# Attention block: first weighted sum in one piece, maxima split by ScalarE and Pool, turn moved from step three to step five

## The reference, cut to what matters

```python
x = x + 0.5 * ffn(layernorm(x), ...)
x = x + attn(layernorm(x), Wq, bq, Wk, bk, Wv, bv, Wo, bo)
x = x + 0.5 * ffn(layernorm(x), ...)
# attn: 32 query heads, 8 key/value heads (4 query heads share one), head size 16
Q, K = rope(Q, K)
scores = einsum('bhqd,bhkd->bhqk', Q, K) / sqrt(16)
w = softmax(scores, axis=-1)
out = einsum('bhqk,bhkd->bhqd', w, V) @ Wo.T + bo
```

## Time and profile before

| | before |
|---|---|
| median of 3 runs | 3099.67 us (3096.92 to 3100.73) |
| the profiled execution | 3102.39 us, of which 3100.6 us is the span |
| mean granted TensorE clock | 0.982 |
| TensorE busy | 2960.6 us, 95% |
| VectorE busy | 1890.7 us, 61% |
| ScalarE busy | 1731.7 us, 56% |
| Pool busy | 749.6 us, 24% |
| attention, first reduction to last output copy | 1005.0 to 2262.3 us |

### The profile page before, as it was taken

One profiled execution on the slowest core, in us unless ns is written; L12 is line 12 of the kernel. 1 busy time (PEld: TensorE's weight loads), 2 busy tenths in 40 slices (PEclk: granted clock), 3 DMA queues, 4 the chain that ended last, 5 costly groups with the idle time before them and its releaser, 6 DMA issues. The chain is left out here.

```text
span 3100.6 us, 61131 instructions
## 1 busy us (share of the span) xinstructions
PE 2960.6 (95%) x20310; PEld 1213.7 (39%) x20310; DVE 1890.7 (61%) x2349; ACT 1731.7 (56%) x3156; POOL 749.6 (24%) x644
## 2 busy tenths in 40 slices
PE   7889999999998999999999999999997999999999
PEld 4444444444564122222222222222233444444444
DVE  7853222221676999999999999999723222222221
ACT  5733333333111599999999999999910333333332
POOL 0154444444443000000000000000022444444444
PEclk9999999999999799999999999999998999999999
DMA  4311110011333011111111111111256011111100
GB/s 132 116 43 41 41 41 14 26 41 42 92 106 102 11 34 31 30 30 30 31 31 30 30 30 30 30 31 31 95 181 227 5 42 41 41 41 41 41 14 28
DMA packets 163902, 160.56 MB, mean 52 GB/s; under 512 B 62552, under 2 KB 100824, under 8 KB 163808
## 3 DMA queue, kind: packets, MB, share of 16 engines
q1 hardware_dynamic: 163808, 159.30, 17.4%
HBM read 111.48 MB, written 47.19 MB: 51 GB/s over the span
## 5 line engine op out<-in xcount | busy, mean ns | idle before, releaser
L1756 DVE TENSOR_REDUCE at_neg_max<-at_max_ps 128x1 f32<-128x1024 f32 x1024 | 1172.6, 1206 | 19.8 <-PE at_max_ps L1634 19.0
L1742 ACT ACTIVATE at_probs<-at_score_ps 128x512 f32<-128x512 f32 x2048 | 1112.9, 597 | 81.9 <-PE at_score_ps L1654 37.8
L1663 PE MATMUL at_out_ps<-at_probs,at_v 128*32 128x256 f32 x8192 | 655.0, 391 | 24.4 <-ACT at_out L1728 24.0
L1634 PE MATMUL at_max_ps<-at_km,at_q 48*128 48x512 f16 x2048 | 633.0, 390 | 13.9 <-PEq L1227 8.2
L1654 PE MATMUL at_score_ps<-at_q,at_ks 50*128 50x512 f16 x2048 | 622.0, 382 | 15.0 <-DMA at_q<-at_max_parts 9.3
L983 DVE SCALAR_TENSOR_TENSOR f_h<-f_up_ps,hr_factor,f_gate 128x512 f32<-128x512 f32 x128 | 96.1, 751 | 478.1 <-ACT f_gate L1057 475.9
L1945 POOL TENSOR_TENSOR rows<-rows,bias 128x512 f32<-128x512 f32 x32 | 39.5, 1265 | 1353.2 <-ACTq L1880 1272.8
L1654 PEld LDWEIGHTS at_score_ps<-at_q,at_ks 50*128 50x128 f16 x2048 | 164.4, 93 | 434.8 <-ACT at_probs L1742 394.7
L413 DVE SCALAR_TENSOR_TENSOR f_h<-f_up_ps,hr_factor,f_gate 128x512 f32<-128x512 f32 x112 | 83.9, 749 | 393.9 <-PE f_up_ps L752 240.8
L1663 PEld LDWEIGHTS at_out_ps<-at_probs,at_v 128*32 128x32 f32 x8192 | 161.6, 108 | 402.1 <-issue 219.7
L1057 ACT ACTIVATE f_gate<-f_gate_ps 128x512 f32<-128x512 f32 x128 | 76.4, 597 | 354.3 <-PE f_up_ps L1130 354.3
(11 more groups left out here) (148 smaller groups left out, 3722.5 us busy)
## 6 DMA issues: line engine op xcount, KB each, us to landing
rows<-x SPq DMA_DIRECT2D x40, 1024.0 KB, 5.6
x<-rows SPq DMA_DIRECT2D x16, 1024.0 KB, 4.6
f_raw<-units SPq DMA_DIRECT2D x48, 256.0 KB, 2.6
at_q<-qk_parts SPq DMA_DIRECT2D x384, 32.0 KB, 1.7
rows<-x SPq DMA_DIRECT2D x32, 256.0 KB, 2.8
at_q<-at_max_parts SPq DMA_DIRECT2D x512, 1.0 KB
att<-at_out SPq DMA_DIRECT2D x256, 32.0 KB
out<-rows SPq DMA_DIRECT2D x8, 1024.0 KB, 4.2
```

The lines of the kernel that those rows point to most:

```text
L1634: done = nc.tensor.matmul(max_ps[u % 2][:, half * QB:(half + 1) * QB], q[k][rows, j // SLOTS, h * QB + c * P:h * QB + (c + 1) * P], km[k][ ...
L1663: last = nc.tensor.matmul(out_ps[2 * HD * j:2 * HD * (j + 1), cols], v[k][:, kc, :], probs[:, kc % PBUF, j, cols], start=(kc == 0 and part ...
L1742: nc.scalar.activation(probs[:, kc % PBUF, j, :], score_ps[pos % RING][:], ACT.Exp, scale=HD ** -0.5).then_inc(exps, 1)
L1756: nc.vector.tensor_reduce(neg_max[:, h, column:column + 1], max_ps[u % 2][:], AX.X, ALU.max, negate=True).then_inc(maxed, 1)
```

## The change

Four edits.

1. The first step's sum of a block is issued in one piece behind the fourth unit of step kc = 1 (before: one part behind its second, one behind its fourth unit). Its wait for `out_copied` moves with it.
2. ScalarE's copy of the previous block's output stands before unit 5 (before: unit 4).
3. The split leaves VectorE. ScalarE copies the turned maxima, scaled, from the bank into a new SBUF tile `max_rows` (16 x 2 x 128, f32) and increments `m_copied`; Pool, which did nothing in the attention, makes the high part and then the low part from it. TensorE's reuse of the bank waits for ScalarE's copy alone; SP's `store_max` waits for Pool.
4. The turn stands before unit 16 (before: unit 8).

ScalarE's last group is written out behind its loop, since it has one turn less.

```diff
-TURN_AT = 2
+TURN_AT = 4
@@ scores
-                    pe.wait_ge(m_split, n + 2)
+                    pe.wait_ge(m_copied, n + 2)
@@ run of TensorE
-                            elif kc >= 1:
-                                if kc == 1 and i == 1:
-                                    pe.wait_ge(out_copied, n + 1)
+                            elif kc == 1 and i == 3:
+                                pe.wait_ge(out_copied, n + 1)
+                                weigh(n, k, 0, 0)
+                                weigh(n, k, 0, 1)
+                            elif kc >= 2:
                                 weigh(n, k, kc - 1, i // 2)
@@ Pool, new
+            for m in range(NG * NB):
+                h = m % NB
+                pool.wait_ge(m_copied, m + 1)
+                nc.gpsimd.tensor_copy(max_parts[:, h, 0, :], max_rows[:, h, :]).then_inc(m_high, 1)
+                pool.wait_ge(m_high, m + 1)
+                nc.gpsimd.tensor_tensor(max_parts[:, h, 1, :], max_rows[:, h, :], max_parts[:, h, 0, :],
+                                        ALU.subtract).then_inc(m_split, 1)
@@ ScalarE
+            def copy_maxima(m, h, ps):
+                act.wait_ge(m_turned, m + 1)
+                if not (isinstance(m, int) and m < NB):
+                    act.wait_ge(m_split, m - 1)
+                nc.scalar.activation(max_rows[:, h, :], ps[0:MU, 0:P], ACT.Copy, scale=1.0 / ANCHOR).then_inc(m_copied, 1)
+
+            copy_maxima(0, 0, score_ps[0])
@@ run of ScalarE
-                            if unit == GH and not (isinstance(n, int) and n == 0):
+                            if unit == GH + 1 and not (isinstance(n, int) and n == 0):
                                 copy_output(n - 1, 1 - h, (G if h else G - 1) * (GH * 32) + 1)
                             act.wait_ge(s_done, n * SU + (unit + 1))
                             nc.scalar.activation(probs[:, kc % PBUF, j, :], score_ps[pos % RING][:], ACT.Exp,
                                                  scale=HD ** -0.5).then_inc(exps, 1)
+                            if unit == TURN_POS and (h == 0 or follow >= 1):
+                                copy_maxima(n + 1, 1 - h, score_ps[TURN_POS % RING])
@@ VectorE
-            def split_maxima(m, h, ps):
-                dve.wait_ge(m_turned, m + 1)
-                nc.vector.tensor_scalar(max_parts[:, h, 0, :], ps[0:MU, 0:P], 1.0 / ANCHOR, None,
-                                        ALU.mult).then_inc(m_high, 1)
-                dve.wait_ge(m_high, m + 1)
-                nc.vector.scalar_tensor_tensor(out=max_parts[:, h, 1, :], in0=ps[0:MU, 0:P], scalar=1.0 / ANCHOR,
-                                               in1=max_parts[:, h, 0, :], op0=ALU.mult,
-                                               op1=ALU.subtract).then_inc(m_split, 1)
```

More of the change, by code:

```diff
@@ L1537, in attention @@
         out = sb("out", [P, NB, QB], F32)
+        max_rows = sb("max_rows", [MU, NB, P], F32)
         anchor = sb("anchor", [2, T], F16)
@@ L1548, in attention @@
         m_turned = sem("m_turned")
+        m_copied = sem("m_copied")
         m_high = sem("m_high")
@@ L1714, in _ @@
                 weigh(NG * NB - 1, 1, KC - 1, part)
+        @block.gpsimd
+        def _(pool):
+            for m in range(NG * NB):
[5 more added lines that the diff above has]
+                                        ALU.subtract).then_inc(m_split, 1)
         @block.scalar
         def _(act):
+            def copy_maxima(m, h, ps):
[4 more added lines that the diff above has]
+            copy_maxima(0, 0, score_ps[0])
             for semaphore, count in before:
@@ L1743, in run @@
                                                  scale=HD ** -0.5).then_inc(exps, 1)
+                            if unit == TURN_POS and (h == 0 or follow >= 1):
+                                copy_maxima(n + 1, 1 - h, score_ps[TURN_POS % RING])
             run(0, 0, 0, 2)
-            with loop(nc, act, 1, NG) as G:
+            with loop(nc, act, 1, NG - 1) as G:
                 run(G, 0, 0, 2)
+            run(NG - 1, 0, 0, 0)
             copy_output(NG * NB - 1, 1, (NG - 1) * (GH * 32) + 1)
@@ L1772, in _ @@
                 for u in range(MU):
-                    if m == 1 and u == 2:
-                        split_maxima(0, 0, score_ps[0])
                     maxima(m, m, u)
@@ L1780, in run @@
                     for u in range(MU):
-                        if u == TURN_AT * MSTEP and (h == 0 or follow >= 1):
-                            split_maxima(n + 1, 1 - h, score_ps[TURN_POS % RING])
                         if follow >= 1:
```

## The result

| | before | after |
|---|---|---|
| median (12 runs each) | 3100.89 us | 3106.38 us |
| lowest to highest | 3096.74 to 3104.39 | 3099.18 to 3111.75 |
| the profiled execution | 3102.39 us, span 3100.6 | 3107.25 us, span 3105.4 |

The ratio is 1.0016, with a 95% interval of 1.0009 to 1.0024: the change makes the kernel some 5.5 us slower. I had forecast 3092.8 us in a range from 3083 to 3105; the median lies 1.4 us above that range.

A forecast was written before the change was run, and what follows sets the result against it. Even blocks were held bound by SP's issues, so only shorter odd blocks help in groups 2 to 29. Terms 5.6 + 0.7 + 0.1 + 0.5 = 6.9 us gave 3095.5, against the median 3092.8; range 3083 to 3105.

The forecast's parts named there:

- no gain or loss by itself: Odd block, turn moved before unit 16: the same matmul, still 0.21 us, so nothing gained or lost.
- Pool's path through SP: Odd block: Pool's pair, SP's 8 issues (4.94 us) and landing end at 17.7 of 18.70 us, hidden with 0.97 spare.
- The sum of the loop: Odd blocks 0.20 us shorter, 18.90 to 18.70, even blocks unchanged; 28 odd blocks give 5.6 us.
- Merged sum: Odd block, units 4 to 8: sum in one piece with the later output copy gains 0.07 us.
- The stall at the sum: TensorE's 0.40 us wait for ScalarE's output copy stays, moved to behind unit 7.
- The rival that it goes: TensorE's stall at the first sum vanishes: up to 0.40 us more in 34 blocks, 3079 us; chance 0.12, shared with shorter even blocks.
- Copy of the maxima: Odd block: ScalarE's copy takes 0.233 us and holds unit 18 to 1.19 behind unit 16, a loss of 0.05.
- the rival of a long copy: ScalarE's copy of the maxima takes up to 0.59 us, holding unit 18 longer: about 3104.5 us; chance 0.14.
- The 0.08 us in units 10 to 16: Odd block, units 10 to 16: excess, put at 0.06 us in the forecast, goes with the split off VectorE.
- The pace of 1.13: Odd block's last six pairs run at VectorE's 1.13 us; split off VectorE makes them 1.11, gaining 0.12.
- a slow Pool: Odd block: Pool's pair takes over 1.7 us, delaying SP's maxima DMAs; at 2.3 about 3111 us; chance 0.10.
- Pool holding up VectorE: Reductions stand still while Pool works, 0.7 us a block; time about 3105 us; chance 0.04.

The follow-up runs named there:

- a_loop: The changed kernel with ScalarE's last group back in its loop and one unread turn more in the last block; 3096.52 us, 0.9986 of before.
- b_peel: The kernel before with only ScalarE's last group written out behind its loop; 3102.53 us, 1.0007 of before.
- a_turn2: The changed kernel with the turn back before unit 8; 3102.70 us, 1.0009 of the kernel before.
- b_turn4: The kernel before with only the turn moved to before unit 16; 3101.80 us, 1.0006 of before.
- b_sum: The kernel before with only the first sum in one piece and ScalarE's output copy before unit 5; 3091.66 us, 0.9973 of before.
- b_split: The kernel before with the split moved to ScalarE and Pool, plus one unread turn in the last block; 3097.89 us, 0.9992 of before.
- b_km_late: The kernel before with SP's key loads for the maxima issued behind the odd block's maxima DMAs; 3083.66 us, 0.9942 of before.
- a_loop_early: The changed kernel, ScalarE's last group in its loop and its copy of the maxima ahead of unit 16's exponential; 3090.19 us, 0.9967 of before.

## Why the prediction was wrong, and where it was right

**The step that failed first: ScalarE's last group, costed at nothing.** The description of the change names it in one sentence ("written out behind its loop"), and my part by part does not have it at all: the sum puts blocks 62 and 63 at 0.1 us gained. It cost 9.9 us (a_loop against the changed kernel, block 63 at 20.56 against 30.46). Of these some 5.4 us are TensorE's wait and the rest the half clock behind it. That writing the group out brings the pause is shown both ways, by a_loop and b_peel. That it is a transfer of code rests on the q14 transfer in each of the three pauses, in b_peel with no other traffic beside it. The pause lasts 5.80 us here against 3.59 and 2.75 because the transfer begins late: 4.0 us into the pause, against 2.1 and 1.2, while from its start to ScalarE's next instruction it is 1.5 to 1.8 us in all three. Why it begins so late is open. SP's loads for the next stage kept the DMA engines about half busy until 2255.2, just when it begins, and b_peel's and a_turn2's pauses did not meet them; no run tests that. Block 62, written out too, has no pause; the pause's place in the code says where it falls, and no run says why there.

**The second: the turn with "no gain or loss by itself", and Pool's path through SP "hidden", with 4.94 us for SP's issues everywhere.** Both held in the loop (b_turn4), where SP had a microsecond to spare as forecast. (The terms shown give 18.70 - 17.68 = 1.02 us to spare, not 0.97.) In block 1 the same 8 issues take 7.5 us, a row of the trace of before that I had not read, since I took block 19 for all. Block 1 takes 1.9 us more for it (1.1 the turn, 0.8 ScalarE and Pool) and block 2, with the clock, 0.7: 2.6 of the 3.7 us of blocks 0 to 3. Of the other 1.1 us, block 0 has 1.3 more, with its full clock 2.1 us later, and block 3 gives 0.2 back. Why SP issues more slowly there no run shows. My sum had neither block 0 nor the clock in it.

**The sum of the loop was right, its terms less so.** Odd blocks gained 0.24 us (forecast 0.20), even ones became 0.05 longer (forecast 0), blocks 4 to 59 gained 5.5 us (forecast 5.6). The two belong together: SP's chain starts at an odd block's last scores, and from there to the next odd block it is 20.24 us before and 20.23 after. Only the stretch from an odd block's first to its last scores counts, and that fell by 0.19 us (17.88 to 17.69); I had counted TensorE's last pair in full.
- Merged sum: from unit 4 to 8 took 2.55 us without the turn, forecast 2.62: the gain is 0.14, not 0.07. The sum follows the copy after 0.05 us and not 0.13. But its true worth is what it does behind unit 8, and alone it is 0.37 (b_sum): I had followed the stall on TensorE and not asked who starves during it.
- The stall at the sum stayed, as I claimed: TensorE's weight loads wait for the output copy 63 times, 0.4 us each. The rival that it goes falls.
- Copy of the maxima: 0.25 us, forecast 0.233, so the rival of a long copy falls; unit 18 comes 1.22 behind unit 16, forecast 1.19. The next pair is late too, 1.18, which I did not have.
- The 0.08 us in units 10 to 16 are not a gain of the split's move: they stay in b_split, which has no split on VectorE. They go where the turn goes (b_turn4: 3.32 there without the turn, and 1.18 in units 18 to 20 in its place). The pace of 1.13 went as forecast, but b_sum shows that it needed no move of the split.
- Pool: 0.28 + 0.42 = 0.70 us, forecast 0.72; SP's issues 11.56 us into block 19, forecast 11.6. The rivals of a slow Pool and of Pool holding up VectorE fall: the three reductions beside Pool's pair in block 19 last 1.22 us each, which is also their mean over the kernel. The Trainium skill's factor of two against VectorE (GPSIMD Engine Reference, Engine selection) is for operations with two inputs, and my estimate of 1.1 us took it for both. It is not reached at this size: the one with two inputs takes 0.42 against VectorE's 0.28, a factor of 1.5, the other 0.28 against 0.27. VectorE read PSUM there and Pool SBUF.
- The even block is bound by SP: b_km_late shows it by 17 us.

**The small stages.** The stretch to block 0 gained 0.4 us (forecast 0.5), block 3 and blocks 60 to 62 together 0.4 (forecast 0.7 with block 1).

So: 3095.5 was my sum; 9.9 for block 63 and 3.7 for blocks 0 to 3 make 3109.1, and with the 2.3 that the last stage happened to take less it is 3106.8, against 3107.25 in that execution. My rival for "slower" was Pool, a mechanism in the loop. None of my cases had a place outside of it, and so the range's upper end was too low.

## What to carry to other kernels

A body written out behind a loop can cost more than the work in it: look for idle "issue" in its first pass and for instruction transfers, and prefer one unread operation more in the loop to a second copy of the body. Work out the loop from one block, but read the first and the last blocks for themselves: a wait hidden in the steady state by a microsecond is open where a queue is slower. When a stall is moved, follow each engine through it: here the gain was that VectorE was no longer starved, and it could be had by the first two edits without the other two; and when one queue makes every second block long, shorten that queue first.

## What the runs showed of the hardware that I had not expected

- ScalarE stood still for 2.75, 3.59 and 5.80 us in code met for the first time behind a loop, each time with an instruction transfer in the pause that began 1.6, 1.5 and 1.8 us before its end; in b_peel it was the only transfer.
- TensorE's granted clock stayed at 1.00 behind waits of 0.9 us (block 20), 1.0 (b_turn4) and 1.28 (a_loop_early), fell to 0.50 for about 3 us behind waits of 1.93 us (block 1 to 2) and 1.98 (a_loop, same place), and to 0.50 for most of the rest of the block behind the waits of block 63 (2.75 us of ScalarE's pause in a_turn2, 5.37 us of TensorE's wait after). In that last block TensorE had no maxima matmuls beside its scores. In block 0 the full clock came back 7.6 us into the block before, 9.8 after and 14.4 in b_sum.
- SP issued the same 8 DMAs in 4.94 us in the loop and in 7.5 to 7.7 us in block 1, before, after, in a_turn2 and in b_turn4.
